# A recurrence step in three passes of split operands, and a reordered end, in a two-layer kernel on one core

## The reference

```
xn = ln(x, norm1); u = xn @ Wu + bu; g = sigmoid(xn @ Wg + bg)
h = 0
repeat 8 times: h = g * (h @ A) + (1 - g) * u
x = x + h
m = gelu(ln(x, norm2) @ mlp_w1 + mlp_b1) @ mlp_w2 + mlp_b2
return x + m
```

## Time and profile before

| | |
|---|---|
| median of 3 runs | 231.0 us (230.25 to 231.27) |
| the profiled execution | 230.03 us, of which the span is 228.2 us |
| TensorE busy | 219.4 us (96% of the span) |
| VectorE busy | 183.1 us (80%) |
| ScalarE busy | 137.5 us (60%) |
| GpSimd busy | 148.9 us (65%) |
| TensorE share of the chain that ended last | 78% |

### The profile page before, as it was taken

One profiled execution on the slowest core, in us unless ns is written; L12 is line 12 of the kernel. 1 busy time (PEld: TensorE's weight loads), 2 busy tenths in 40 slices (PEclk: granted clock), 3 DMA queues, 4 the chain that ended last, 5 costly groups with the idle time before them and its releaser, 6 DMA issues.

```text
span 228.2 us, 4139 instructions
## 1 busy us (share of the span) xinstructions
PE 219.4 (96%) x1332; PEld 182.2 (80%) x1332; DVE 183.1 (80%) x462; ACT 137.5 (60%) x309; POOL 148.9 (65%) x179
## 2 busy tenths in 40 slices
PE   8999796999999999999999999999999999999985
PEld 5696665889898979787987688788888888788784
DVE  7799999999999998995168986978796958586641
ACT  5766784878787766756744395546264563515352
POOL 6564786778889877949677374666658472927230
PEclk9999999999999999999999999999999999999999
DMA  4861000000000000000000012030404032021012
GB/s 110 212 195 40 1 0 0 4 0 0 3 1 0 3 1 0 3 0 0 0 3 0 1 70 72 34 105 34 138 4 146 27 102 73 34 73 34 0 40 66
DMA packets 11973, 9.31 MB, mean 41 GB/s; under 512 B 1232, under 2 KB 11696, under 8 KB 11952
## 3 DMA queue, kind: packets, MB, share of 16 engines
q1 hardware_dynamic: 11664, 8.97, 13.1%
q10 hardware_dynamic: 288, 0.09, 0.2%
HBM read 5.31 MB, written 3.74 MB: 40 GB/s over the span
## 4 chain that ended last, share of the span: by engine, by line
PE 78%; DVE 11%; DMA 5%; SPq 2%; issue 1%; ACT 1%; POOL 0%; DVEq 0%
PE bank L1407 12%; PE pA L1407 9%; PE pM L1700 9%; PE pM L1358 8%; PE bank L1532 7%; DMA x_all<-in_x 5%; DVE cA L1073 4%; DVE cB L1073 2%; PE bank L1575 2%; PE bank L1474 2%; PE bank L1580 2%; PE pA L1445 2%; PE bank L1457 2%; PE pM L1350 2%; PE pM L1346 2%; PE pM L1347 2%
## 5 line engine op out<-in xcount | busy, mean ns | idle before, releaser
L426 POOL TENSOR_TENSOR rs<-var,power 128x4 f32<-128x4 f32 x32 | 32.5, 1015 | 22.5 <-DVE var L964 18.8
L1073 DVE SCALAR_TENSOR_TENSOR cA<-pA,cols,cA 128x528 f32<-128x528 f32 x54 | 40.7, 754 | 0.2
L1700 PEld LDWEIGHTS pM<-w,hid 128*128 128x128 f32 x192 | 29.7, 191 | 5.6 <-ACT hid L916 1.2
L1358 PEld LDWEIGHTS pM<-w,hid 128*128 128x128 f32 x192 | 28.4, 191 | 5.7 <-issue 1.0
L1153 DVE SCALAR_TENSOR_TENSOR q<-th,bank 96x256 f32<-96x256 f32 x48 | 19.2, 412 | 13.3 <-PE bank L1407 13.3
L1700 PE MATMUL pM<-w,hid 128*128 128x96 f32 x192 | 28.8, 267 | 0.8 <-ACT hid L916 0.8
L1358 PE MATMUL pM<-w,hid 128*128 128x96 f32 x192 | 28.9, 266 | 0.0
L1407 PE MATMUL pA<-q,a_half 96*96 96x256 f32 x96 | 27.0, 380 | 0.2 <-DVE q L1153 0.2
L1073 DVE SCALAR_TENSOR_TENSOR cB<-bank,cols,cB 128x256 f32<-128x256 f32 x56 | 26.4, 472 | 0.0
L559 POOL TENSOR_TENSOR xl<-xt,xh 96x512 fp32r<-96x512 f32 x11 | 14.1, 1283 | 17.1 <-ACT xh L894 17.1
L1532 PE MATMUL bank<-local,mix 128*128 128x384 f32 x64 | 24.8, 497 | 0.1
(11 more groups left out here) (249 smaller groups left out, 608.5 us busy)
## 6 DMA issues: line engine op xcount, KB each, us to landing
moved<-blocks SPq DMA_DIRECT2D x11, 192.0 KB, 1.9
xt<-moved SPq DMA_DIRECT2D x33, 64.0 KB, 2.0
x_all<-in_x SPq DMA_DIRECT2D x8, 192.0 KB, 2.9
out<-y SPq DMA_DIRECT2D x7, 192.0 KB, 2.1
w<-in_w SPq DMA_DIRECT2D x1, 480.0 KB, 5.8
w<-in_w SPq DMA_DIRECT2D x1, 336.0 KB, 3.5
mix<-in_mix SPq DMA_DIRECT2D x1, 256.0 KB, 3.7
out<-y SPq DMA_DIRECT2D x2, 96.0 KB, 1.7
```

Of the source, the lines that this page charges most:

```text
L426: pool.tensor_tensor(rs[:, :], var[:, :], power[:, :], ALU.pow).then_inc(step, 1)
L1073: dve.scalar_tensor_tensor(out=acc, in0=src, scalar=col(f"k{'AB'[grp]}{k}"), in1=acc, op0=ALU.mult, op1=ALU.add).then_inc(s["conv_step"], 1)
L1358: last = pe.matmul(psum[:, k * D:(k + 1) * D], hid[:, j * TILE + k * P:j * TILE + (k + 1) * P], wc0("w2", j * D, (j + 1) * D), start=(j == ...
L1700: last = pe.matmul(dst, hid1[:, j * TILE + k * P:j * TILE + (k + 1) * P], wc1("m2", j * D, (j + 1) * D), start=j == 0 and (k == 0 if whole ...
```

## The change

There are three parts.

In tiles 1 to 7, step 5 of the recurrence (`SPLIT_STEP`) is no f32 product any more. ScalarE writes the fp32r high part `q_high` of each half, VectorE writes `q_low = q - q_high` (two SBUF inputs, 96x256), and TensorE sums `a_high * q_high`, `a_low * q_high` and `a_high * q_low`. `a_high` and `a_low` are made once, in `turn`, by ScalarE and GpSimd.

In `body1(8)` the `h_transposes` of tile 7 go ahead of `m1(0)` of tile 6. The second product of tile 6 goes to bank 3 (`V_BESIDE`), so that it doesn't wait for `store_sum` of tile 5; `M1_LAST` moves to bank 4 for that. VectorE normalizes two chunks of `xn4` of tile 7 and ScalarE two, and GpSimd's `x4b` of that tile waits until they are done.

In `body1(9)` the twelve places of `m2` of tile 7 are reordered, so that its first half (chunks 0 and 1) is finished after six places.

```diff
-M1_LAST = (2, 3, 1)
+M1_LAST = (2, 4, 1)
+V_BESIDE = 3
+SPLIT_STEP = 5
...
 GpSimd
+                pool.wait_ge(s["a_high_ready"], 1)
+                pool.tensor_tensor(a_low[0:D, :], a_half[0:D, :], a_high[0:D, :].bitcast(F32), ALU.subtract)\
...
                     pool.wait_ge(s["x4_ready"], x4_count(m))
+                    if is_last(m):
+                        pool.wait_ge(s["xn4_ready"], 4 * m + 4)
                     add_row(x4b[m % 2][:, :], x4[:, :], rows[:, 2 * D:3 * D], s["x4b_ready"])
...
 ScalarE
-                        scale_rows(xn4, x4, rs4, s["xn4_ready"], range(3))
+                        scale_rows(xn4, x4, rs4, s["xn4_ready"], range(2))
...
+            def split_q_high(c):
+                if tile_known(c):
+                    for h in range(2):
+                        act.wait_ge(s["q_ready"], QS * c + 2 * SPLIT_STEP + h - 1)
+                        if c > 1:
+                            act.wait_ge(s["step_done"], HALF_STEPS * (c - 1) + 2 * SPLIT_STEP + h + 1)
+                        act.activation(q_high[0:D, half(h)], moved(c, SPLIT_STEP)[0:D, half(h)], ACT.Copy)\
+                           .then_inc(s["q_high_ready"], 1)
...
                 gelu(2)
+                split_q_high(c)
                 evac_gu(f)
...
 VectorE
-                for k in (3,):
+                for k in (2, 3):
...
+            def split_q_low(c):
+                if tile_known(c):
+                    for h in range(2):
+                        dve.wait_ge(s["q_high_ready"], 2 * (c - 1) + h + 1)
+                        dve.wait_ge(s["q_ready"], QS * c + 2 * SPLIT_STEP + h - 1)
+                        dve.tensor_tensor(q_low[0:D, half(h)], moved(c, SPLIT_STEP)[0:D, half(h)],
+                                          q_high[0:D, half(h)].bitcast(F32), ALU.subtract).then_inc(s["q_low_ready"], 1)
...
-                    store_sum(g)
+                    store_sum(g, V_BESIDE)
...
                 step(c, 4)
+                split_q_low(c)
                 ln3_stats(i + 3)
                 step(c, 5)
...
 TensorE
+            def split_step(c, h):
+                if tile_known(c):
+                    if c == 1:
+                        pe.wait_ge(s["a_high_ready"], 1)
+                        pe.wait_ge(s["a_low_ready"], 1)
+                    dst = step_bank(SPLIT_STEP, h)
+                    pe.wait_ge(s["q_high_ready"], 2 * (c - 1) + h + 1)
+                    pe.matmul(dst, a_high[0:D, :], q_high[0:D, half(h)], start=True, stop=False, skip_group_check=True)
+                    pe.matmul(dst, a_low[0:D, :], q_high[0:D, half(h)], start=False, stop=False, skip_group_check=True)
+                    pe.wait_ge(s["q_low_ready"], 2 * (c - 1) + h + 1)
+                    pe.matmul(dst, a_high[0:D, :], q_low[0:D, half(h)], start=False, stop=True, skip_group_check=True)\
+                      .then_inc(s["step_done"], 1)
...
                                 if u == 0:
                                     pe.wait_ge(s["x3_ready"], TILES)
-                                else:
+                                elif is_last(u):
+                                    pe.wait_ge(s["y_ready"], u - 1)
+                                elif not ln4_beside(u):
                                     pe.wait_ge(s["y_ready"], u)
...
-                    m2(g, *range(12))
+                    m2(g, 0, 1, 4, 5, 8, 9, 2, 3, 6, 7, 10, 11)
...
                 if is_last(m):
+                    h_transposes(m)
                     m1(0)
-                    h_transposes(m)
...
                 for h in range(2):
-                    rec_step(c, 5, [h])
+                    split_step(c, h)
                     m2(g, 4 + h)
```

More of the change, by code:

```diff
@@ L194, in build @@
         q_one, q_three = sb("q_one", TILE), sb("q_three", TILE)
+        a_high, a_low = sb("a_high", D, F32R), sb("a_low", D, F32R)
+        q_high, q_low = sb("q_high", TILE, F32R), sb("q_low", TILE, F32R)
         h8 = sb("h8", TILE)
@@ L220, in build @@
             "gu_ready", "step_done", "hs_first", "q_ready", "hs_step", "h8_ready", "trh_done", "x4_ready",
-            "bn4_step", "var4_ready", "ln4_step", "xn4_ready", "x4b_ready", "tr4_done", "x4_copied", "x4_split", "x4_lo",
+            "bn4_step", "var4_ready", "ln4_step", "xn4_ready", "x4b_ready", "a_high_ready", "a_low_ready", "q_high_ready", "q_low_ready", "tr4_done", "x4_copied", "x4_split", "x4_lo",
             "hid1_psum", "gelu1_done", "m2_done", "y_ready", "y_stored")}
@@ L582, in turn @@
                 ln3_std(3)
+                pool.wait_ge(s["a_high_ready"], 1)
+                pool.tensor_tensor(a_low[0:D, :], a_half[0:D, :], a_high[0:D, :].bitcast(F32), ALU.subtract)\
+                    .then_inc(s["a_low_ready"], 1)
             def body1(i):
@@ L902, in turn @@
                 normalize3(2)
+                act.activation(a_high[0:D, :], a_half[0:D, :], ACT.Copy).then_inc(s["a_high_ready"], 1)
             def body1(i):
@@ L1183, in turn, with store_sum @@
                 last_h(0)
-            def store_sum(p):
+            def store_sum(p, at=V_BANK):
                 dve.wait_ge(s["x4b_ready"], p + 1)
@@ L1188, in store_sum @@
                 dve.wait_ge(s["m2_done"], p + 1)
-                dve.tensor_tensor(y[:, :], bank[V_BANK][:, 0:384], x4b[p % 2][:, :], ALU.add).then_inc(s["y_ready"], 1)
+                dve.tensor_tensor(y[:, :], bank[at][:, 0:384], x4b[p % 2][:, :], ALU.add).then_inc(s["y_ready"], 1)
             def body1(i):
@@ L1694, in m2 @@
                                     pe.wait_ge(s["x3_ready"], TILES)
-                                else:
+                                elif is_last(u):
+                                    pe.wait_ge(s["y_ready"], u - 1)
+                                elif not ln4_beside(u):
                                     pe.wait_ge(s["y_ready"], u)
                             whole = not is_last(u)
-                            dst = bank[V_BANK][:, k * D:(k + 1) * D] if whole else \
+                            dst = bank[V_BESIDE if ln4_beside(u) else V_BANK][:, k * D:(k + 1) * D] if whole else \
                                 bank[(V_BANK, 7)[k // 2]][:, (k % 2) * D:(k % 2 + 1) * D]
```

## The result

The changed kernel takes 233.24 us (median of 4 runs, 232.95 to 233.51) against 230.62 us before (4 runs, 230.21 to 231.27). The ratio is 1.012, with a 95% interval of 1.0097 to 1.0143: slower by 2.6 us. The forecast was 234.2 us against a median of 231.0, 3.2 us slower, with a range of 229.4 to 235.5. The profiled execution is 233.22 us long and its span 231.4; before it was 228.2. The difference of the spans is 3.2 us.

What follows compares the result with a forecast made beforehand. TensorE, busy 96% of the span, was taken as the bound, with VectorE work free only in its gap. Tiles +4.05 us and end -0.7 gave 233.4 profiled, median 234.2; range 229.4 to 235.5, own range 232.7 to 235.5.

Steps and rivals of the forecast that it cites:

- 0.71 us for six passes: TensorE's step 5: six fp32r passes priced like w_in_b, 0.71 us instead of 0.86.
- the guess that it works in the other order too: Between steps 4 and 5: VectorE's two-SBUF-input q_low waits until GpSimd's running addition ends, 149.30 in tile 2.
- The second guess: Between q_low's halves on VectorE: GpSimd's waiting x4b goes in for 1.01 us, delaying the second half to 150.99.
- Rival 2: Split step: exclusion, but VectorE keeps the ports for both q_low halves; 230.7 us, no change; chance 0.16.
- rival 1: Split step: no exclusion with GpSimd first, q_low hidden in VectorE's gap; 229.7 us, faster; chance 0.20.
- VectorE's idle time in tile 2: VectorE between steps 4 and 5: its idle time lies in this one place, 1.17 us.
- tiles 2 to 4 against 1.0 forecast: TensorE's step 6 in tiles 2 to 4 comes 1.0 us late net in each.
- tiles 5 and 6 against 0.3: Tiles without ln3_stats: TensorE's step 6 comes 0.3 us late in each.
- the table load: Tile 1: q_high queues behind ScalarE's table load until 136.72, costing 0.35 us.
- the meeting of `a_low` with `last_h` of tile 0: In the turn: making a_low may meet last_h, at worst 0.3 us; counted as nothing.
- the step that gave the 0.80 us to the bank: End: own bank removes TensorE's 0.80 us idle before tile 6's second product; the end gives 0.7 us net.
- the distance from the profiled execution to the median: Added to the profiled forecast of 233.4 us: 1.0 us, giving a median of 234.3, stated as 234.2.

Runs made afterwards that it cites:

- The first run: Changed kernel with q_low's second input taken from step 4's PSUM bank instead of q_high in SBUF, computing other data; 228.60 us, ratio 0.991 to the kernel before.
- the run with one subtraction: Changed kernel with both halves of q_low in one 96x512 subtraction; 230.46 us, ratio 0.9983 to the kernel before.
- the end alone: Changed kernel with only the reordered end kept, step 5 one f32 product in all tiles; 229.65 us against 230.56 before, ratio 0.9958.
- the end without its bank: Reordered end only, f32 step 5, with the old bank for tile 6's second product; 229.81 us against 230.46 before, ratio 0.9969.
- the run with GpSimd's order: Changed kernel with GpSimd's x4b ahead of add_q(c, 3), which waits in tiles 2 to 7 for both q_low; 230.44 us, ratio 0.9976.

## Why the prediction was right

**TensorE's work.** 0.71 us for six passes was taken from `w_in_b`. Three passes take 0.35, so 0.70; and where nothing is late (tiles 2 to 6 of the run with the PSUM input) a tile is 0.17 us shorter, against 0.15 forecast.

**The exclusion.** The case rested on one GpSimd instruction of 1.45 us and the guess that it works in the other order too. The first run shows it: with one SBUF input the same instruction takes 0.41 us beside the same GpSimd sum, with two it takes 1.03 in tile 2 of the changed kernel, and the one that meets `x4b` 1.23. The rule of the Trainium skill (SBUF — State Buffer, "Who interferes with whom") that speaks of two SBUF inputs agrees with both. The second guess, that `x4b` goes in between the halves, is in the changed kernel's timeline and priced by the run with one subtraction. Rival 2 (both halves in one lock) would have cost what that run costs, and rival 1 (no exclusion) what the PSUM run costs: 230.7 and 229.7 were forecast for them and 230.5 and 228.6 measured, the second 1.1 us less than forecast. Two smaller things were off. TensorE idles 0.51 us before step 6, not near 1: step 6 is less late than forecast, and a part of the delay is spent inside step 5, where TensorE waits for `q_low`. And VectorE's idle time in tile 2 wasn't in one place: beside the 1.17 us there were 0.21 between the halves of step 5 and 0.47 before a transpose, but nothing hung on that.

**The sum, term by term.** Without the share of `last_h` (0.10 in tile 2, 0.31 in tile 3, 0.19 in tile 4, 0.31 in tile 5) the rows of the table give 0.80, 0.83 and 0.81 for tiles 2 to 4 against 1.0 forecast, and 0.10 and 0.09 for tiles 5 and 6 against 0.3. Both were sized too high for one reason: the sum gave each waiting instruction its full length after the one that held it up. In tile 2 each subtraction ends 0.28 us after the addition that it waits for, not 0.34, `x4b` ends 0.87 after the first subtraction, not 1.01, and step 5 starts 0.65 after the second one, not 0.83. (The 0.83 isn't what the earlier trace rows show, either: from 148.37 to 149.32 is 0.95, of which `var` waits 0.12.) Tiles 5 and 6 have the subtractions and `x4b` alone, and were over by 0.2.

Tile 1 costs 0.56, of which 0.35 was forecast for the table load (its own numbers, 138.7 less 138.16 less 0.15, give 0.39). The other 0.2 is the meeting of `a_low` with `last_h` of tile 0, two instructions of which take 0.94 us instead of 0.75; it was named with a price of up to 0.3 and counted as nothing. Both are gone in the version that leaves tile 1 unsplit, where it takes 13.16 us (128.75 to 141.91) as before. Tile 7 costs 0.15 against 0.1. The meeting of `last_h` with GpSimd's split of the returning tile, 0.91 in all, was missing: it needed the question of what VectorE would run into once it was late. So the mechanism was right, but that the sum came out at 4.13 against 4.05 is luck: 0.9 that was left out stands against 1.0 that was too much in tiles 2 to 6.

**The end.** The total was 0.7 against 0.91 to 0.93 measured, just outside the 0.4 to 0.9 that it was given. `m1(0)` at 214.55 is where the end alone has it, too, though its step 6 comes 0.13 later than before. But the step that gave the 0.80 us to the bank was wrong. What it gives by itself is 0.24, since `xn4` is next in line and comes hardly sooner. The rest of the end gives 0.69 without the bank, and the bank adds 0.22 on top. No run changes the order of the transposes alone, but the profile of the end without its bank points to it: the product starts 4.92 us after step 6 instead of 5.60, behind an earlier `y`, which is all of the 0.69, and `xn4` is ready at 217.93, 0.6 us before it is wanted. The prediction had all the times for this in hand: it checked `xn4` against the reordered end, and didn't ask what `y` would do there.

**The difference to the median.** The forecast of 234.2 was 1.0 us too high, and that is not the sum, which gave 233.4 for the profiled execution where 233.22 was measured. It is the 1.0 us that was added for the distance from the profiled execution to the median: here the two are 0.02 us apart. Against before, 3.2 us more was forecast and 2.6 measured, 3.2 in the spans; the median of before itself fell by 0.4 with one more run. The stated range, 229.4 to 235.5, was wide enough for rival 1 as well; the result lies in the forecast's own range of 232.7 to 235.5, too.

## What to carry to other kernels

Idle time of an engine isn't room for any instruction: before an instruction with two SBUF inputs goes into a gap of VectorE, look at what GpSimd reads from SBUF in that gap, and count each such instruction to the end of the GpSimd instruction that it meets, with one more slipping in between two in a row. The cheapest cure here was the place of an operand: a result that is read only once can stay in PSUM. And when an idle time ends with a release, compute what is next in line before counting it as a gain, as with the bank.

## What the runs showed of the hardware

Exclusion between VectorE and GpSimd is seen in both orders: GpSimd's addition of 1.01 us takes 1.19 when it waits for a subtraction, and VectorE's two-input subtraction of 0.41 us up to 1.23 when it waits for the addition. Of VectorE's instructions, those that waited were the ones with two SBUF inputs and some TENSOR_SCALAR with one tensor input: the tiny `var` (128x4, 0.17 us alone, up to 0.81 beside GpSimd's `hs` in the run with GpSimd's order) and `xn` (128x96, 1.00 us beside `x4b` in the kernel before). Those with a PSUM input among two didn't wait in these traces, nor did the statistics (0.35 us) and STREAM_TRANSPOSE (0.58 us), which read SBUF alone. VectorE read a product from a PSUM bank and wrote to other columns of the same bank as fast as to SBUF: two halves of step 4 take 0.77 us in tile 2 of the versions that do so, and 0.76 in the changed kernel.
